# Weighing the low-rank product of a language-model tower: one VectorE product against a ScalarE copy and a GpSimd product, with GpSimd's normalising behind VectorE's gate

## The chip, the core and the metric

The kernel runs on one core of a Trainium2 chip. The time is the device time of one execution in microseconds (us), taken as the median of several runs. The engines are called by their names or by the profile's short ones: PE is TensorE (matmuls; PEld its weight loads), DVE is VectorE, ACT is ScalarE, POOL is GpSimd, and SP is SyncE, which here only issues DMAs.

## What is computed

32 sequences of 512 tokens, width 128, everything in float32. The embedding of the tokens gives h; then h = h + attention(layernorm(h)) with 8 heads of width 16, and h = h + experts(layernorm(h)). The change sits in the experts. Cut to what matters, with xf the normalised input (`softmax` over the 4 experts e):

```python
gate_logits = softmax(xf @ gate_w.T)
adapted = gate_logits - sigmoid(xf @ thr_w.T) / e
weights = adapted * (adapted >= 0)
weights = weights / sum(weights)                  # 1 where the sum is 0
hidden = relu(einsum('ni,ehi->neh', xf, fc1_w))
lo = einsum('neh,ehr->ner', hidden, lora_A)       # rank 16 for each expert
lo = einsum('ner,ero->neo', lo, lora_B)
out = einsum('ne,ned->nd', weights, einsum('neo,edo->ned', lo, fc2_w))
```

## The kernel before

`tower` keeps one pipeline going over the 32 sequences. Each engine has its own program, and all of them walk through the same steps t = -5 to 34. In step t the attention scores of sequence t are made, while other sequences are in other stages: the work that belongs to sequence t+k is listed with its offset k. So (-3) is the end of the experts of sequence t-3, (-2) the gate and the first expert product of t-2, (-1) the last part of the attention of t-1, (+3) the queries and keys of t+3.

A step has 16 slots c. PE does in each slot two score tiles for the softmax (`scores_T`, L724, into a ring `sc` of 3 PSUM banks), two score tiles whose row maxima are wanted ahead of time (`scores`, L750, into `mix`, 4 PSUM banks), one product from the table `PRODUCTS`, and in every fourth slot 16 matmuls with the values (`values`, L737). Its order is fixed by `PE_ORDER`. The low-rank product `low` (L809) is that of slot 3, the turning `xn2T` (L762) that of slot 5, and the experts' output `out` (L825) that of slot 6. A bank of `mix` is written again four uses later, and PE waits there for whoever reads it last (`mix_user`, `mix_free`). A bank of the ring is written three tiles later, when ACT's exponential of the tile before has been done (`ring_free`).

The other engines follow tables that say after which tile of the step each piece of work stands, and each engine executes in that order:

- ACT (`ACT_WORK`): 32 exponentials (`exp`, L592) a step. Ahead of the one of slot 4 stand the bias and the bfloat16 cast of the queries and of the keys of t+3 (`copy_qk`, L596 and L600, four instructions) and the copy of the second half of the attention's result of t-1 (`copy_ctx`, L616).
- DVE (`DVE_WORK`): 32 row maxima (`row_max`, L1025) a step. In slot 3 stand the embedding's add, half of its statistics and `weigh` (L1099), which reads the low-rank product from PSUM, multiplies it by the gate weights `wrow` and writes `low`. In slot 7 stand `finish` (L1104), the last add of sequence t-3, and `invert_den` (L1044), the reciprocal of the softmax's denominators of t-1. In slots 9 and 10 stands the gate of t-2: some ten small instructions between SBUF tiles, of which `gsm` (L1071), `gad` (L1074), `gsel` (L1080), `wsafe` (L1087) and the last, `wts` (L1092), are named below.
- POOL (`POOL_WORK`): among others `norm2` (L491, L495), then five products that cut the queries and keys into three bfloat16 pieces (`second`, L485, comes first), then `normalise` (L528 twice, L532), which multiplies the attention's result by the reciprocals.
- SP (`SP_WORK`) issues the DMAs in one queue. Those of interest go ahead of each other in this order: two pieces of 128 KB (L339), the denominators out to DRAM (`den_out`, L369), a third piece, the denominators back in (`den_in`, L385), ..., the reciprocals out and in again (`rden_out`, `rden_in`, L392 and L400), ..., and at the end of the step `stack`, the six loads of queries and keys of t+3 from DRAM (L356, L363), some 1.5 MB.

The chain of the denominators therefore is, within one step: `values` of slot 3, `copy_ctx` on ACT, `den_out`, `den_in`, `invert_den` on DVE, `rden_out`, `rden_in`, `normalise` on POOL, and in the next step's slot 0 the product `project` (L787) on PE.

A wait is written `upto(engine, semaphore, b, n)`: until n signals have come for every sequence up to b.

## Time and profile before

| | |
|---|---|
| median of 3 runs | 1127.43 us (1126.55 to 1129.59) |
| the profiled execution's own time | 1126.86 us |
| its span, first to last instruction | 1125.1 us |
| PE busy | 1040.1 us, 92% |
| DVE busy | 948.8 us, 84% |
| ACT busy | 807.0 us, 72% |
| POOL busy | 682.1 us, 61% |
| mean granted PE clock | 0.962 of full speed |

The profile is that of one execution. Starts are counted from the start of the span. A row of the timeline may join several like instructions (x4); what stands in brackets behind it is the time in which the engine was idle before it, and what ended that wait.

### The profile page before, as it was taken

Reading aid. Unit: us, or ns where it says so; the run is one execution under the profiler, and the core shown is the slowest. Engines: PE = TensorE matmul, PEld = TensorE weight load, DVE = VectorE, ACT = ScalarE, POOL = GpSimd, SP = SyncE. Lnnn points to the kernel's source line nnn. Section 1 sums busy time; section 2 is a strip of 40 time slices with the busy share of each in tenths; the row PEclk is TensorE's granted clock in tenths of the full one; section 3 lists DMA queues with packets and bytes.
Section 4 is the critical chain, followed back from the end, with each engine's and each line's share of the span. In section 5 each row is a group of like instructions: output and inputs, shape, how many; then the busy total and the mean of one; then the engine's idle time right before and its main releaser. Section 6 shows DMA issues by size and latency. Waiting matters only on the chain.

```text
span 1125.1 us, 20263 instructions
## 1 busy us (share of the span) xinstructions
PE 1040.1 (92%) x6158; PEld 407.9 (36%) x6158; DVE 948.8 (84%) x2442; ACT 807.0 (72%) x1578; POOL 682.1 (61%) x684
## 2 busy tenths in 40 slices
PE   4368999999999999999999999999999999989865
PEld 2112233333434434343433443434343343333322
DVE  7498899999989989899999999999999998887312
ACT  2217787777877788787877778778787777856731
POOL 1855676677666666677666666667766666621231
PEclk9558999999999999999999999999999999999997
DMA  2553645555554445555555545565555554541111
GB/s 74 148 135 89 137 106 135 129 137 127 137 130 124 126 121 130 142 127 134 126 137 126 126 121 132 130 143 126 137 125 137 128 126 113 121 96 36 55 50 32
DMA packets 93530, 132.43 MB, mean 118 GB/s; under 512 B 18205, under 2 KB 69918, under 8 KB 87398
## 3 DMA queue, kind: packets, MB, share of 16 engines
q1 hardware_dynamic: 91872, 129.54, 47.9%
q10 hardware_dynamic: 1550, 1.59, 0.6%
q8 instruction: 50, 0.82, 0.3%
q14 instruction: 58, 0.48, 0.1%
HBM read 89.20 MB, written 35.01 MB: 110 GB/s over the span
## 4 chain that ended last, share of the span: by engine, by line
PE 64%; DVE 16%; DMA 6%; ACT 5%; issue 2%; POOL 1%; SPq 1%; POOLq 0%; ACTq 0%; DVEq 0%
PE pv L737 17%; PE mix L750 15%; PE sc L724 13%; DVE negmax L1025 9%; PE mix L804 7%; DMA den_dram<-ctx_sb 4%; PE mix L787 3%; DVE bn L1015 2%; ACT probs L592 2%; PE mix L809 2%; DVE h L1050 2%; PE mix L825 2%; DMA den<-den_dram 2%; ACT qk L596 1%; PE mix L769 1%
## 5 line engine op out<-in xcount | busy, mean ns | idle before, releaser
L1025 DVE TENSOR_REDUCE negmax<-mix 128x1 f32<-128x512 f32 x1024 | 649.0, 679 | 56.8 <-PE mix L750 56.2
L592 ACT ACTIVATE probs<-sc 128x512 f32<-128x512 f32 x1024 | 556.3, 600 | 118.2 <-PE sc L724 112.0
L724 PE MATMUL sc<-qstk,kstk 120*128 120x512 bf16 x1024 | 364.2, 382 | 5.6 <-ACT probs L592 4.9
L750 PE MATMUL mix<-kstk,qstk 96*128 96x512 bf16 x1024 | 331.7, 395 | 24.6 <-DMA kstk<-stack_dram 7.3
L737 PE MATMUL pv<-probs,vals 128*32 128x512 f32 x2048 | 244.8, 595 | 0.0
L528 POOL TENSOR_TENSOR ctxh<-ctx_sb,rdenb 128x512 f32<-128x512 f32 x64 | 81.0, 1268 | 245.3 <-DMA rdenb<-rden_dram 244.5
L750 PEld LDWEIGHTS mix<-kstk,qstk 96*128 96x128 bf16 x1024 | 89.4, 98 | 266.5 <-DVE negmax L1025 76.1
L724 PEld LDWEIGHTS sc<-qstk,kstk 120*128 120x128 bf16 x1024 | 100.1, 98 | 107.5 <-ACT probs L592 33.4
L804 PE MATMUL mix<-xn2T,fc1T_sb 128*128 128x512 f32 x256 | 138.2, 622 | 0.7 <-ACT hid L646 0.7
L508 POOL TENSOR_TENSOR qk<-qk,rstdb 128x512 f32<-128x512 f32 x64 | 81.1, 1269 | 57.9 <-DMA rstdb<-rstd_dram 53.4
L737 PEld LDWEIGHTS pv<-probs,vals 128*32 128x32 f32 x2048 | 59.1, 109 | 117.4 <-issue 100.1
L646 ACT ACTIVATE hid<-mix 128x512 f32<-128x512 f32 x128 | 76.5, 598 | 31.2 <-PE mix L804 28.7
L502 POOL TENSOR_TENSOR pieces<-qkr,pieces 128x512 bf16<-128x512 f32 x64 | 74.0, 1156 | 8.5
L485 POOL TENSOR_TENSOR pieces<-qk,pieces 128x512 bf16<-128x512 f32 x64 | 74.0, 1156 | 6.6 <-ACT pieces L600 6.6
L479 POOL TENSOR_TENSOR qkr<-qk,pieces 128x512 f32<-128x512 f32 x64 | 74.1, 1159 | 0.0
L460 POOL TENSOR_TENSOR rstd<-ve,minus_half 128x4 f32<-128x4 f32 x64 | 64.9, 1013 | 5.0
L458 POOL TENSOR_TENSOR ve<-mv,eps_sb 128x4 f32<-128x4 f32 x64 | 12.9, 201 | 73.8 <-DVE mv L1021 71.1
L804 PEld LDWEIGHTS mix<-xn2T,fc1T_sb 128*128 128x128 f32 x256 | 43.9, 191 | 36.7 <-DVE negmax L1025 24.7
L605 ACT COPY v<-mix 128x512 f32<-128x512 f32 x32 | 18.8, 586 | 46.8 <-POOL vals L520 39.1
L474 POOL TENSOR_TENSOR hb_sb<-h_sb,obias 128x512 f32<-128x512 f32 x32 | 40.5, 1265 | 15.0 <-DVE h L1050 14.8
L1010 DVE TENSOR_TENSOR qk<-mix,posQK 128x512 f32<-128x512 f32 x64 | 43.4, 679 | 7.1 <-POOL qkr L479 6.6
L1050 DVE TENSOR_TENSOR h<-mix,hb_sb 128x512 f32<-128x512 f32 x32 | 22.1, 692 | 28.6 <-PE mix L787 27.5
(141 smaller groups left out, 1088.5 us busy)
## 6 DMA issues: line engine op xcount, KB each, us to landing
stack_dram<-pieces SPq DMA_DIRECT2D x192, 128.0 KB
rdenb<-rden_dram SPq DMA_DIRECT2D x64, 256.0 KB
qstk<-stack_dram SPq DMA_DIRECT2D x31, 384.0 KB, 6.6
kstk<-stack_dram SPq DMA_DIRECT2D x31, 384.0 KB, 8.8
rstdb<-rstd_dram SPq DMA_DIRECT2D x32, 256.0 KB, 3.4
wrow<-w_dram SPq DMA_DIRECT2D x32, 256.0 KB
out<-out_sb SPq DMA_DIRECT2D x32, 256.0 KB, 2.6
qstk<-stack_dram SPq DMA_DIRECT2D x31, 256.0 KB, 7.0
```

The source lines that it names most:

```text
L479: pool.tensor_tensor(qkr[:, side, :], qk32[:, side, :], pieces[:, side, 0, :], ALU.subtract).then_inc(s_res0, 1)
L485: pool.tensor_tensor(pieces[:, side, 1, :], qk32[:, side, :], pieces[:, side, 0, :], ALU.subtract).then_inc(s_pc1, 1)
L502: pool.tensor_tensor(pieces[:, side, 2, :], qkr[:, side, :], pieces[:, side, 1, :], ALU.subtract).then_inc(s_pc2, 1)
L508: pool.tensor_tensor(qk32[:, side, :], qk32[:, side, :], rstdb[:], ALU.mult).then_inc(s_scaled, 1)
L528: pool.tensor_tensor(ctxh[:, g, :], ctx_sb[:, u % 2, g, :], rdenb[:, g, :], ALU.mult).then_inc(s_ctxh, 1)
L592: act.activation(probs[:, c % 8, i % 2], sc[:, i % RING], ACT.Exp).then_inc(s_exp, 1)
L646: act.activation(hid[:, e, :], aux(f"fc1_{e}", 1), ACT.Relu).then_inc(s_hid, 1)
L724: pe.matmul(sc[:, i % RING, :], kstk[0:KROWS, u, h, j * P:(j + 1) * P], qstk[0:KROWS, u, h, :], start=True, stop=True).then_inc(s_score, 1)
L737: mm = pe.matmul(pv[Q * i:Q * i + Q, :], vals[:, u, 2 * half + jj, 4 * g + i, :], probs[:, 4 * (r % 2) + i, jj, :], start=(half == 0 and j ...
L750: pe.matmul(max_bank(m), qstk[0:STK, u, h, j * P:(j + 1) * P], kstk[0:STK, u, h, :], start=True, stop=True).then_inc(s_mxmm, 1)
L804: pe.matmul(aux(f"fc1_{e}", 1), fc1T_sb[:, e, :], xn2T[:], start=True, stop=True).then_inc(s_fc1mm, 1)
L1025: dve.tensor_reduce(negmax[:, m // NT, m % NT:m % NT + 1], max_bank(m), AX.X, ALU.max, negate=True).then_inc(s_max, 1)
```

## The change

VectorE's `weigh` goes. ScalarE gets `copy_low` ahead of the queries' bias in slot 4: it copies the low-rank product from PSUM to `low`. GpSimd gets `weigh` behind `norm2`: it multiplies `low` in place by `wrow`. The new semaphore `s_lowcp` stands between the two, and PE's wait for the bank of `mix` that held the product is now on it. Apart from that, `normalise` of sequence b on GpSimd now first waits until the gate of b-1 is complete on VectorE (13 signals), except for the last sequence. The rest of the arithmetic and all DMAs are the same.

```diff
--- before.py
+++ after.py
@@ -61,7 +61,7 @@
 BEFORE, BEHIND = (3, 7), (11,)
 
 ACT_WORK = [
-    (1, 1, "relu", -3, 3), (4, 0, "qk", 3, 0), (4, 0, "qk", 3, 1), (4, 0, "ctx", -1, 1), (6, 0, "xn2T", -2, 0),
+    (1, 1, "relu", -3, 3), (4, 0, "low", -3, 0), (4, 0, "qk", 3, 0), (4, 0, "qk", 3, 1), (4, 0, "ctx", -1, 1), (6, 0, "xn2T", -2, 0),
     (8, 0, "gates", -2, 0), (9, 1, "gate_exp", -2, 0), (9, 1, "relu", -2, 0), (10, 1, "relu", -2, 1),
     (12, 0, "rT", 4, 0), (12, 0, "wT", -2, 0), (12, 0, "mT", 1, 0), (12, 1, "ctx", 0, 0), (13, 1, "relu", -2, 2),
     (15, 2, "v", 4, 0),
@@ -69,14 +69,14 @@
 
 DVE_WORK = [
     (0, 1, "add_attention", -2, 0), (1, 0, "stats2", -2, 0), (1, 1, "stats2", -2, 1), (2, 0, "moments2", -2, 0),
-    (3, 1, "add_pos", 4, 0), (3, 1, "stats1", 4, 0), (3, 1, "weigh", -3, 0), (6, 0, "stats1", 4, 1),
+    (3, 1, "add_pos", 4, 0), (3, 1, "stats1", 4, 0), (6, 0, "stats1", 4, 1),
     (6, 1, "moments1", 4, 0), (7, 1, "finish", -3, 0), (7, 1, "invert_den", -1, 0),
     (9, 0, "gate", -2, 0), (10, 1, "gate", -2, 1), (10, 1, "gate", -2, 2), (10, 1, "gate", -2, 3),
     (13, 0, "add_qk", 4, 0), (15, 1, "add_qk", 4, 1), (15, 1, "hot", 5, 0),
 ]
 
 POOL_WORK = [
-    ("scale", 3, 0), ("add_bias", 3, 0), ("scale", 3, 1), ("rstd2", -2, 0), ("norm2", -2, 0),
+    ("scale", 3, 0), ("add_bias", 3, 0), ("scale", 3, 1), ("rstd2", -2, 0), ("norm2", -2, 0), ("weigh", -3, 0),
     ("second", 3, 0), ("residual", 3, 0), ("third", 3, 0), ("second", 3, 1), ("rstd1", 4, 0),
     ("residual", 3, 1), ("third", 3, 1), ("normalise", -1, 0), ("v", 3, 0),
 ]
@@ -287,6 +287,7 @@
         s_wTmm, s_wT, s_wout, s_win = sem("s_wTmm"), sem("s_wT"), sem("s_wout"), sem("s_win")
         s_fc1mm, s_hid = sem("s_fc1mm"), sem("s_hid")
         s_lomm, s_low = sem("s_lomm"), sem("s_low")
+        s_lowcp = sem("s_lowcp")
         s_outmm, s_out, s_store = sem("s_outmm"), sem("s_out"), sem("s_store")
 
         def upto(eng, s, b, per=1, k=None):
@@ -523,6 +524,8 @@
 
             def normalise(b, u):
 
+                if b < NSEQ - 1:
+                    upto(pool, s_gate, b - 1, 13)
                 for g in range(2):
                     upto(pool, s_rdin[g], b, 16)
                     pool.tensor_tensor(ctxh[:, g, :], ctx_sb[:, u % 2, g, :], rdenb[:, g, :],
@@ -531,6 +534,11 @@
                 upto(pool, s_projmm, b - 1)
                 pool.tensor_tensor(ctxn[:], ctxh[:, 0, :], ctxh[:, 1, :], ALU.add).then_inc(s_ctxn, 1)
 
+            def weigh(b):
+                upto(pool, s_lowcp, b)
+                upto(pool, s_win, b, 16)
+                pool.tensor_tensor(low[:], low[:], wrow[:], ALU.mult).then_inc(s_low, 1)
+
             pool.wait_ge(s_setcp, 4)
             pool.wait_ge(s_const, 3)
 
@@ -539,6 +547,7 @@
                 "rstd2": lambda b, u, _: rstd_second(b),
                 "scale": lambda b, u, side: scale(b, side),
                 "v": lambda b, u, _: value(b, u),
+                "weigh": lambda b, u, _: weigh(b),
                 "residual": lambda b, u, side: residual(b, side),
                 "second": lambda b, u, side: second(b, side),
                 "third": lambda b, u, side: third(b, side),
@@ -635,6 +644,11 @@
                 upto(act, s_wout, b - 1, 16 * WREP)
                 act.copy(wT, aux("mT", 1)[Q:Q + NT * NE, 0:P]).then_inc(s_wT, 1)
 
+            def copy_low(b):
+                upto(act, s_lomm, b)
+                upto(act, s_outmm, b - 1)
+                act.copy(low[:], aux("low", 1)).then_inc(s_lowcp, 1)
+
             def copy_rT(b):
                 upto(act, s_rTmm, b)
                 upto(act, s_rstdout, b - 1, 16)
@@ -651,6 +665,7 @@
                 "xn2T": lambda b, u, _: copy_xn2T(b),
                 "relu": lambda b, u, e: relu(b, e),
                 "wT": lambda b, u, _: copy_wT(b),
+                "low": lambda b, u, _: copy_low(b),
                 "rT": lambda b, u, _: copy_rT(b),
                 "mT": lambda b, u, _: copy_mT(b),
                 "ctx": lambda b, u, g: copy_ctx(b, g, u),
@@ -837,7 +852,7 @@
                 "fc1_2": (lambda b: fc1(b, 2), (s_hid, NE, 3)),
                 "fc1_3": (lambda b: fc1(b, 3), (s_hid, NE, 4)),
                 "embed": (embed, (s_h, 1, 1)),
-                "low": (low_rank, (s_low, 1, 1)),
+                "low": (low_rank, (s_lowcp, 1, 1)),
                 "mT": (turn_max, (s_mT, 1, 1)),
                 "project": (project, (s_h2, 1, 1)),
                 "out": (experts_out, (s_out, 1, 1)),
@@ -1092,12 +1107,6 @@
                 dve.tensor_tensor(wts[:, 0:NT], gsel[:], wrec[:].unsqueeze(2).broadcast_to([P, NT, NE]),
                                   ALU.mult).then_inc(s_gate, 1)
 
-            def weigh(b):
-                upto(dve, s_lomm, b)
-                upto(dve, s_win, b, 16)
-                upto(dve, s_outmm, b - 1)
-                dve.tensor_tensor(low[:], aux("low", 1), wrow[:], ALU.mult).then_inc(s_low, 1)
-
             def finish(b, u):
                 upto(dve, s_outmm, b)
                 upto(dve, s_store, b - 1, 16)
@@ -1119,7 +1128,6 @@
                 "stats2": lambda b, u, half: stats(b, h2[:, b % H2], bn2, s_h2, s_bn2, half),
                 "moments2": lambda b, u, _: moments(b, bn2, mv2, s_bn2, s_mv2),
                 "gate": lambda b, u, part: (gate_first, gate_second, gate_third, gate_fourth)[part](b),
-                "weigh": lambda b, u, _: weigh(b),
                 "finish": lambda b, u, _: finish(b, u),
             }
```

ACT, in a step of the steady part, from the end of slot 3 to slot 4 (L592 and L601 are the exponentials, L596/L605 and L600/L609 the queries' and keys' bias and cast, L616/L625 `copy_ctx`). Before:

```order
L592 ACTIVATE probs<-sc 128x512 x5
L596 ACTIVATE qk<-qk,qb_sb 128x512
L600 CAST pieces<-qk 128x512
L596 ACTIVATE qk<-qk,qkb_sb 128x512
L600 CAST pieces<-qk 128x512
L616 COPY ctx_sb<-pv 128x512
L592 ACTIVATE probs<-sc 128x512 x4
L621 COPY xn2T<-mix 128x512
```

And with the change:

```order
L601 ACTIVATE probs<-sc 128x512 x5
L650 COPY low<-mix 128x512
L605 ACTIVATE qk<-qk,qb_sb 128x512
L609 CAST pieces<-qk 128x512
L605 ACTIVATE qk<-qk,qkb_sb 128x512
L609 CAST pieces<-qk 128x512
L625 COPY ctx_sb<-pv 128x512
L601 ACTIVATE probs<-sc 128x512 x4
L630 COPY xn2T<-mix 128x512
```

The new copy stands ahead of four instructions for the queries and keys, of `copy_ctx` and of the exponentials of slot 4 and later.

POOL, the middle of a step (L495/L496 is the end of `norm2`, L528/L531 and L532/L535 are `normalise`). Before:

```order
L491 TENSOR_TENSOR xn<-h,mv 128x512
L495 TENSOR_TENSOR xn<-xn,rstd 128x512
L485 TENSOR_TENSOR pieces<-qk,pieces 128x512
L479 TENSOR_TENSOR qkr<-qk,pieces 128x512
L502 TENSOR_TENSOR pieces<-qkr,pieces 128x512
L485 TENSOR_TENSOR pieces<-qk,pieces 128x512
L458 TENSOR_TENSOR ve<-mv,eps_sb 128x4
L460 TENSOR_TENSOR rstd<-ve,minus_half 128x4
L479 TENSOR_TENSOR qkr<-qk,pieces 128x512
L502 TENSOR_TENSOR pieces<-qkr,pieces 128x512
L528 TENSOR_TENSOR ctxh<-ctx_sb,rdenb 128x512 x2
```

And with the change:

```order
L492 TENSOR_TENSOR xn<-h,mv 128x512
L496 TENSOR_TENSOR xn<-xn,rstd 128x512
L540 TENSOR_TENSOR low<-low,wrow 128x512
L486 TENSOR_TENSOR pieces<-qk,pieces 128x512
L480 TENSOR_TENSOR qkr<-qk,pieces 128x512
L503 TENSOR_TENSOR pieces<-qkr,pieces 128x512
L486 TENSOR_TENSOR pieces<-qk,pieces 128x512
L459 TENSOR_TENSOR ve<-mv,eps_sb 128x4
L461 TENSOR_TENSOR rstd<-ve,minus_half 128x4
L480 TENSOR_TENSOR qkr<-qk,pieces 128x512
L503 TENSOR_TENSOR pieces<-qkr,pieces 128x512
L531 TENSOR_TENSOR ctxh<-ctx_sb,rdenb 128x512 x2
```

Eight instructions, and with them the pieces' stores on SP, come after the new product.

## Rows read from the trace of the kernel before

**Rows 1.** The page: busy time of each engine (us, share, instructions)
```profile
PE 1040.1 (92%) x6158; PEld 407.9 (36%) x6158; DVE 948.8 (84%) x2442; ACT 807.0 (72%) x1578; POOL 682.1 (61%) x684
```
**Rows 2.** Timeline of PE, `low` in six steps: start, us, what [idle before]
```profile
176.16 1.06 PE L809 MATMUL mix<-hid,loA_sb 128*32 128x512 f32 x8
...
490.18 1.06 PE L809 MATMUL mix<-hid,loA_sb 128*32 128x512 f32 x8
...
521.35 1.06 PE L809 MATMUL mix<-hid,loA_sb 128*32 128x512 f32 x8
...
553.02 1.06 PE L809 MATMUL mix<-hid,loA_sb 128*32 128x512 f32 x8
...
991.24 1.07 PE L809 MATMUL mix<-hid,loA_sb 128*32 128x512 f32 x8
...
1026.03 1.06 PE L809 MATMUL mix<-hid,loA_sb 128*32 128x512 f32 x8
```
**Rows 3.** Timeline of DVE, the reciprocal in two of those steps
```profile
500.23 0.35 DVE L1044 RECIPROCAL rden<-den 128x32 f32<-128x32 f32 x1 [0.70 <-DMA den<-den_dram]
...
532.07 0.35 DVE L1044 RECIPROCAL rden<-den 128x32 f32<-128x32 f32 x1 [1.35 <-DMA den<-den_dram]
```
**Rows 4.** Timeline of all engines, slots 3 and 4 of one step
```profile
615.69 1.07 PE L809 MATMUL mix<-hid,loA_sb 128*32 128x512 f32 x8
...
616.43 0.72 ACT L596 ACTIVATE qk<-qk,qb_sb 128x512 f32<-128x512 f32 x1
...
617.66 1.04 POOL L495 TENSOR_TENSOR xn<-xn,rstd 128x512 f32<-128x512 f32 x1
...
617.87 0.67 DVE L1099 TENSOR_TENSOR low<-mix,wrow 128x512 f32<-128x512 f32 x1
...
618.83 3.16 DVE L1025 TENSOR_REDUCE negmax<-mix 128x1 f32<-128x512 f32 x5 [0.29 <-PE mix L750]
...
618.99 0.58 ACT L616 COPY ctx_sb<-pv 128x512 f32<-128x512 f32 x1
...
619.47 2.21 ACT L592 ACTIVATE probs<-sc 128x512 f32<-128x512 f32 x4
...
619.84 0.52 SPq L369 DMA_DIRECT2D den_dram<-ctx_sb  x1
...
620.67 0.38 PE L724 MATMUL sc<-qstk,kstk 120*128 120x512 bf16 x1
...
621.54 1.05 PE L825 MATMUL mix<-exp_w,low 128*128 128x128 f32 x8
```
**Rows 5.** The page's groups: `normalise`'s two products, busy and mean ns | idle before
```profile
L528 POOL TENSOR_TENSOR ctxh<-ctx_sb,rdenb 128x512 f32<-128x512 f32 x64 | 81.0, 1268 | 245.3 <-DMA rdenb<-rden_dram 244.5
```
**Rows 6.** Timeline of SP, `stack`'s last loads and the denominators in two steps
```profile
611.44 1.58 SPq L363 DMA_DIRECT2D kstk<-stack_dram  x3
...
624.46 0.34 SPq L385 DMA_DIRECT2D den<-den_dram  x1
...
994.70 0.56 SPq L369 DMA_DIRECT2D den_dram<-ctx_sb  x1
998.75 0.34 SPq L385 DMA_DIRECT2D den<-den_dram  x1
```
**Rows 7.** The chain that ended last, the denominators' store in step 32
```profile
1082.72 1.69 DMA den_dram<-ctx_sb
```
**Rows 8.** Timeline, gate against `normalise` in step 29 (and the last row in step 30)
```profile
1007.20 2.58 POOL L528 TENSOR_TENSOR ctxh<-ctx_sb,rdenb 128x512 f32<-128x512 f32 x2 [12.94 <-DMA rdenb<-rden_dram]
1007.23 1.27 DVE L1071 TENSOR_TENSOR gsm<-lexp,grec 128x16 f32<-128x16 f32 x1
...
1011.63 0.41 PE L814 MATMUL mix<-id,wts 128*32 128x128 f32 x2 [2.62 <-DVE wts L1092]
...
1043.99 0.41 PE L814 MATMUL mix<-id,wts 128*32 128x128 f32 x2 [0.85 <-DVE wts L1092]
```
**Rows 9.** Timeline of DVE, `weigh` in the last step
```profile
1118.73 0.69 DVE L1099 TENSOR_TENSOR low<-mix,wrow 128x512 f32<-128x512 f32 x1 [7.41 <-DMA wrow<-w_dram]
```

## The prediction

> **What bounds the kernel now.** I read the busy shares first. PE is at 92% and DVE at 84%, ACT and POOL far below [rows 1], so PE sets the pace and the question is what still makes it wait. A 26-step stretch of the pipeline runs from `low` of step 3 to `low` of step 29: 991.24 - 176.16 = 815.1 us, or 31.35 us a step [rows 2].
>
> Then I compared steps. `low` to `low` is 31.17 in one step and 31.67 in the next [rows 2]. Eight of the 26 steps lie within 0.01 of 31.18, and none is shorter: a floor. The reciprocal of the denominators begins 500.23 - 490.18 = 10.05 after `low` in the step at the floor, and 532.07 - 521.35 = 10.72 in the long one [rows 2, 3]. DVE idles for the denominators in both, 0.70 and 1.35 [rows 3]. So a step lasts 31.18, and longer by what the reciprocal comes later than about 10.72 - 0.50 = 10.22. Two things can therefore lengthen a step: PE's own stream, and the chain of the denominators. Spare time elsewhere buys nothing.
>
> **DVE loses `weigh`: worth nothing.** 32 x 0.67 us = 21.5 us of DVE work go [rows 4]. But behind it DVE idles 0.29 us until PE delivers the next score tile [rows 4], and before the reciprocal it idles again [rows 3]. Without `weigh` the first of these gaps grows to about 0.96, and the row maxima start at the same moment. The bank of `mix` comes free earlier (about 617.4 against 618.54), but PE wants it only for the second row-max tile of slot 4, after 619. I cost the removal at zero. If that cover were gone, it would be worth up to 26 x 0.17 = 4.4 us, the excess over the floor.
>
> The Trainium skill says otherwise, in "Perfetto Trace Analysis", section "Optimizing Scalar/DVE Operations": where DVE is saturated, moving work to Scalar or even GPSIMD may pay. It would make this edit a gain, and is the third rival below. The 0.29 us of idle time behind `weigh` speak against DVE being saturated here.
>
> **ACT gains a copy, at a bad place.** `low` ends at 616.76 on PE; DVE's response to PE is some hundredths, so the copy starts at about 616.82, where the queries' bias started at 616.43 [rows 4]. A copy of this shape holds ACT for 619.47 - 618.99 = 0.48 before the next instruction starts [rows 4]. Everything behind it then starts at 617.30, later by 0.86. Two customers are behind it.
>
> First, PE's ring. The exponential of slot 4 would start at 620.33 and, with some 0.60 for one of them, end at 620.93; PE needs that for the score tile that it now starts at 620.67 [rows 4]. That tile comes at about 620.99: 0.32 later, less than the 0.86 because the ring had slack. The next tiles need later exponentials and fit behind the shifted stream. PE's stream from here to the reciprocal shows no wait in which 0.32 could vanish, so I let the floor rise to 31.50. Over 26 steps that is at least 26 x (0.32 - 0.17) = 3.9 us, more in the five steps that already lie above 31.50 (the denominators set their length, so they gain nothing and lose nothing; by their excess over 31.50, 0.7 in all): **+4.6 us**. Bounds: 0 if PE absorbs it, 26 x 0.32 = 8.3 if the two delays add.
>
> Second, `copy_ctx` and with it `den_out`, which would be issued at 620.70 instead of 619.84. Here I had to choose. `den_in` follows it after 624.46 - 619.84 = 4.62 us [rows 4, 6]. In step 32, without other traffic, the same store takes 1.69 [rows 7]. So some 2.9 us of the 4.62 are waiting in the DMA queues, behind the six big loads issued until 613.0 [rows 6] and two pieces. Step 29 separates the causes: no pieces are stored there, `den_out` goes out at 3.46 after `low` instead of 4.15, and still `den_in` comes only at 998.75 - 991.24 = 7.51 instead of 8.77 [rows 2, 4, 6]. Its latency, 4.05, is still far above 1.69, so the backlog of the loads sets the landing, not the issue. With the later issue the store would still be queued before that backlog is gone (620.70 + 1.69 = 622.4, against 624.46). I take a shift of **0** for the landing; the other end is the full 0.86, which the rivals price.
>
> The Trainium skill's "DMA: Bandwidth & Descriptors", section "Anatomy of one DMA", speaks against this choice: a fixed cost of about 2 us, most of it the write receipt from the target, plus bytes over bandwidth. By that a store of 8 KB lands a constant time after its issue, so 0.86 later, and the sum would be that of the first rival. The unloaded 1.69 agrees with the page, the 4.62 and 4.05 do not.
>
> **POOL gains a product, in idle time.** It costs 1.27 us like the two-input product of `normalise` [rows 5]. `norm2` ends at 618.70, so it runs until about 619.97, and its input, the copy, is there by 617.4. `out` on PE starts at 621.54 [rows 4]: 1.5 us to spare. The cutting of the pieces moves 1.27 later, and the first of the POOL pieces goes to SP behind `den_out`, ahead of `den_in`: it would be ready at about 621.2 and issued before 622, still before 624.46. POOL then waits for the reciprocals, 244.5 us in all over 32 sequences, 7.6 a step [rows 5]; the 1.27 come out of that. If the cover were gone, it would be 26 x 1.27 = 33 us. I cost it at zero.
>
> **POOL's `normalise` waits for the gate.** In the steady steps the reciprocals arrive after the gate is done, so the wait costs nothing, or a few tenths that `project` does not feel. In steps 29 and 30 it is the other way round. No pieces delay the denominators there, `normalise` starts in the middle of the gate, and the gate's `gsm` takes 1.27 us, exactly the time of POOL's product beside it [rows 8]. PE then waits 2.62 for the gate's result, and 0.85 in step 30 [rows 8]. Step 29 lasts 1026.03 - 991.24 = 34.79, 3.61 above the floor [rows 2], although it lacks the products `q`, `k`, `v` and `embed`. Behind the wait those two steps should be clean. I take -4.0 for step 29 (between 2.6, PE's wait alone, and some 4.5, the excess plus the missing products) and -0.85 for step 30: **-4.9 us**. `normalise` itself moves by 1.5 us there, and `project` follows only in the next step.
>
> **The drain.** In the last step `weigh` starts when its weights land [rows 9] and PE waits for it: 1.27 - 0.69 = +0.6. In the two steps before, `weigh` on POOL stands behind `norm2`, and `out` on PE stands between the turning and the gate's matmuls; it comes between 0 and 0.7 later, since only the turning's matmuls are beside the product. I take 0.35 twice. **+1.3 us**. In steps 29 to 31 ACT has no queries and keys to cast and waits for PE there, so the copy is covered.
>
> **Sum:** 4.6 - 4.9 + 1.3 = +1.0 us. The profiled execution took 1126.86 us (span 1125.1 and 1.8 around it), which gives 1127.9. That execution lies 0.57 below the median of the three runs, so for a median I say 1128.4.
>
> **Rivals.**
>
> 1. The denominators land 0.86 later. The queue is not what holds the small store, or the later pieces push into a gap in front of it. Then DVE's reciprocal moves from a mean of about 10.3 to 11.1 after `low`, and a step lasts 31.18 + 0.9 = 32.1 instead of 31.35: 26 x 0.73 = +19, in all 19.0 - 4.9 + 1.3 = +15.4, or 1143. It decides from a shift of the landing of some 0.1 us on. For it: in both rows the landing is later in the step where the store is issued later. Against it: the backlog above.
> 2. The gate's wait gives nothing, because the collision moves instead of going, or the tail is short of something else. Then +4.9 comes back: 1133. Against it: the overlap is exactly what the wait forbids.
> 3. The relief counts and ACT's copy is absorbed. The ring's stall does not appear: 0 - 4.9 + 1.3 = -3.6, or 1124. If the missing `weigh` also lets DVE run ahead and takes the 4.4 us of excess with it, 1119.5. For it: DVE is busy 84% [rows 1]. Against it: the 0.29, and that the reciprocal waits for a DMA.
> 4. The change does less than it says: the queries' bias starts hardly later (ACT overlaps the copy with it), and the collisions in the tail had their cause in the load of that one execution, not in the order. Then nothing is left but the drain, +1.3: 1129.
>
> **Chances.** My forecast with cases around it 0.50 (its own range 1124 to 1133); rival 1 0.15; rival 2 0.08; rival 3 0.22; rival 4 0.05. A measurement of this kernel can tell about 0.3%, 3.4 us, from no change: 1124.0 to 1130.8 is the same. Of the forecast 0.34 lies inside, 0.05 below and 0.11 above; of rival 3 0.17 below and 0.05 inside; rival 4 inside; rivals 1 and 2 above. That gives faster 0.22, same 0.44, slower 0.34. The range leaves out no more than 2 in 10: it runs from 1120, which drops the lower form of rival 3, to 1140, which drops most of rival 1's full form.
>
> **What would show it.** The floor of `low` to `low` at about 31.5 instead of 31.18, with PE's score tile of slot 5 at 5.3 after `low` instead of 4.98. `den_out` near 5.0 after `low`, but `den_in` still at 8.4 to 8.8. DVE idle for about 0.95 us before the row maxima of slot 3. POOL's product ending near 4.3, with `out` unmoved apart from the 0.3. No gate instruction longer than some 0.2 us, and step 29 at about 31. A `den_in` near 9.5 would prove rival 1, an unchanged floor rival 3.

## The result and the profile after

The changed kernel takes 1133.31 us (median of 6 runs, 1131.26 to 1134.42), the kernel before beside it 1127.38 (1125.41 to 1129.59): a ratio of 1.0051, 95% interval [1.0037, 1.0065]. It is slower by half a per cent. That lies in the range (1120 to 1140), 4.9 us above the forecast and just outside what I had called the same.

The page's line on the engines shows the change as planned: DVE lost 24.5 us of work, POOL gained 37.6 and ACT 11.6 (against [rows 1]).

```profile
PE 1046.3 (92%) x6158; PEld 406.3 (36%) x6158; DVE 924.3 (82%) x2410; ACT 818.6 (72%) x1610; POOL 719.7 (64%) x716
```

The timeline of PE, `low` in six steps (start, us, what), answers to [rows 2]:

```profile
176.24 1.07 PE L824 MATMUL mix<-hid,loA_sb 128*32 128x512 f32 x8
...
460.82 1.06 PE L824 MATMUL mix<-hid,loA_sb 128*32 128x512 f32 x8
...
493.31 1.06 PE L824 MATMUL mix<-hid,loA_sb 128*32 128x512 f32 x8
...
524.82 1.07 PE L824 MATMUL mix<-hid,loA_sb 128*32 128x512 f32 x8
...
1001.12 1.07 PE L824 MATMUL mix<-hid,loA_sb 128*32 128x512 f32 x8
...
1031.89 1.07 PE L824 MATMUL mix<-hid,loA_sb 128*32 128x512 f32 x8
```

The 26 steps take 1001.12 - 176.24 = 824.9 us where they took 815.1. A step at the floor lasts 524.82 - 493.31 = 31.51, and the long one ahead of it 493.31 - 460.82 = 32.49. Step 29 is down from 34.79 to 30.77. Of every trace I took this sum, the same way:

| profiled execution | 26 steps | of it 26 floors | above the floor | step 29 | step 30 | from `low` of step 31 on | span |
|---|---|---|---|---|---|---|---|
| before | 815.1 | 810.7 | 4.4 | 34.79 | 29.42 | 69.6 | 1125.1 |
| after | 824.9 | 819.3 | 5.6 | 30.77 | 28.33 | 72.4 | 1132.6 |
| difference | +9.8 | +8.6 | +1.2 | -4.0 | -1.1 | +2.8 | +7.5 |

(The start up to the first `low` is 0.1 later. The profiled execution of after, 1134.42 by its own time, is 1.1 above its median.)

The timeline of all engines over slots 3 and 4 of the step whose `low` starts at 620.40, against [rows 4]:

```profile
620.40 1.07 PE L824 MATMUL mix<-hid,loA_sb 128*32 128x512 f32 x8
...
621.53 0.59 ACT L650 COPY low<-mix 128x512 f32<-128x512 f32 x1 [0.28 <-PE mix L824]
...
622.02 0.72 ACT L605 ACTIVATE qk<-qk,qb_sb 128x512 f32<-128x512 f32 x1
...
622.37 1.04 POOL L496 TENSOR_TENSOR xn<-xn,rstd 128x512 f32<-128x512 f32 x1
...
623.37 1.27 POOL L540 TENSOR_TENSOR low<-low,wrow 128x512 f32<-128x512 f32 x1
...
623.54 2.48 DVE L1040 TENSOR_REDUCE negmax<-mix 128x1 f32<-128x512 f32 x4 [0.89 <-PE mix L765]
...
624.57 0.58 ACT L625 COPY ctx_sb<-pv 128x512 f32<-128x512 f32 x1
...
625.42 0.52 SPq L370 DMA_DIRECT2D den_dram<-ctx_sb  x1
...
625.71 0.39 PE L739 MATMUL sc<-qstk,kstk 120*128 120x512 bf16 x1 [0.17 <-ACT probs L601]
...
626.59 1.05 PE L840 MATMUL mix<-exp_w,low 128*128 128x128 f32 x8
...
628.35 0.34 SPq L386 DMA_DIRECT2D den<-den_dram  x1
```

Relative to `low`: the queries' bias starts at 1.62 (before 0.74), `copy_ctx` at 4.17 (3.30), `den_out` at 5.02 (4.15), PE's score tile at 5.31 (4.98) and `out` at 6.19 (5.85). Ahead of that tile PE now waits for an exponential; the view gives 0.17 of idle time for it, the tile itself starts 0.33 later. `den_in` goes out at 7.95 here, at 8.37 in the mean of the 26 steps (before 8.48). DVE idles 0.89 ahead of the row maxima (before 0.29).

Two steps differ in the reciprocal, in DVE's timeline:

```profile
472.35 0.35 DVE L1059 RECIPROCAL rden<-den 128x32 f32<-128x32 f32 x1 [1.83 <-DMA den<-den_dram]
...
503.18 0.35 DVE L1059 RECIPROCAL rden<-den 128x32 f32<-128x32 f32 x1 [0.17 <-DMA den<-den_dram]
```

The first comes 11.53 after its `low`, the second 9.87. The DMA view of 469.5 to 472.4, in the long step (queue, kind: packets, MB, share; then an issue with KB and us to landing), shows what differs:

```profile
q8 instruction: 1, 0.02, 2.3%
...
den<-den_dram SPq DMA_DIRECT2D x1, 16.0 KB, 2.8
```

And of 501.4 to 503.2, in the step at the floor; it has no line for q8:

```profile
den<-den_dram SPq DMA_DIRECT2D x1, 16.0 KB, 1.7
```

The same read of the denominators takes 2.8 us to land in the one and 1.7 in the other. The one has beside its read a packet of queue 8, 16 KB of instructions, that starts at 470.09; the other has none. The page counts 50 of these packets in 1132.6 us. A narrower DMA view, 470.05 to 470.25, holds this packet and nothing else, with this share of 16 engines' 0.2 us, which is 1.05 us on one of them:

```profile
q8 instruction: 1, 0.02, 32.7%
```

The 50 packets of this trace take 0.88 to 2.06 us, 1.14 in the mean.

The read gives 16 landing signals, one for each part of it. In the long step 15 of them have come by 1.60 us after the issue, and the last comes at 2.82. It is so in all eight steps of the 26 that have such a packet beside the read: 14 of the 16 are there by 1.65, and the last comes at 2.00 to 3.39. In the other 18 steps the last comes at 1.54 to 1.81. What is late is one part of the read, in one step two, and not the whole.

The gate in step 29, against [rows 8], in the timeline: `normalise` starts when `wts` is done, the gate's `gsm` takes 0.18 instead of 1.27, and PE's turning stands there without a wait.

```profile
1017.11 0.18 DVE L1086 TENSOR_TENSOR gsm<-lexp,grec 128x16 f32<-128x16 f32 x1
...
1018.59 0.30 PE L829 MATMUL mix<-id,wts 128*32 128x128 f32 x1
1018.61 2.49 POOL L531 TENSOR_TENSOR ctxh<-ctx_sb,rdenb 128x512 f32<-128x512 f32 x2 [13.25 <-DVE wts L1107]
```

The last step, against [rows 9]: the weights land, POOL's product takes 1.26 instead of 0.69, and PE waits 4.10 instead of 3.0.

```profile
1125.72 1.26 POOL L540 TENSOR_TENSOR low<-low,wrow 128x512 f32<-128x512 f32 x1 [14.89 <-DMA wrow<-w_dram]
1127.13 2.04 PE L840 MATMUL mix<-exp_w,low 128*128 128x128 f32 x8 [4.10 <-POOL low L540]
```

### The profile page after: what moved, and what is told of

Read it like the earlier page. It is cut to its first block, busy times and chain, and to the rows that moved or that the text cites. A ratio compares the mean times of both kernels' runs of the same rounds, so it can differ in the third digit from the quotient of the medians.

```text
span 1132.6 us, 20356 instructions
## 1 busy us (share of the span) xinstructions
PE 1046.3 (92%) x6158; PEld 406.3 (36%) x6158; DVE 924.3 (82%) x2410; ACT 818.6 (72%) x1610; POOL 719.7 (64%) x716
## 4 chain that ended last, share of the span: by engine, by line
PE 59%; DVE 15%; ACT 8%; DMA 5%; issue 5%; POOL 2%; SPq 1%; POOLq 0%; ACTq 0%
PE pv L752 14%; PE mix L765 13%; PE sc L739 12%; DVE negmax L1040 9%; PE mix L819 8%; ACT qk L605 4%; PE mix L824 3%; PE mix L802 3%; DMA den_dram<-ctx_sb 2%; ACT probs L601 2%; DVE bn L1030 2%; PE mix L840 2%; DMA den<-den_dram 2%; DVE h L1065 2%; PE mix L784 1%
## 5 line engine op out<-in xcount | busy, mean ns | idle before, releaser
L601 ACT ACTIVATE probs<-sc 128x512 f32<-128x512 f32 x1024 | 550.3, 603 | 124.2 <-PE sc L739 121.5
L765 PE MATMUL mix<-kstk,qstk 96*128 96x512 bf16 x1024 | 330.3, 394 | 26.9 <-DVE negmax L1040 7.8
L531 POOL TENSOR_TENSOR ctxh<-ctx_sb,rdenb 128x512 f32<-128x512 f32 x64 | 80.4, 1266 | 212.5 <-DMA rdenb<-rden_dram 144.5
L765 PEld LDWEIGHTS mix<-kstk,qstk 96*128 96x128 bf16 x1024 | 88.4, 98 | 268.4 <-DVE negmax L1040 78.2
L540 POOL TENSOR_TENSOR low<-low,wrow 128x512 f32<-128x512 f32 x32 | 40.7, 1271 | 14.9 <-DMA wrow<-w_dram 14.9
L1113 DVE TENSOR_TENSOR out_sb<-mix,h 128x512 f32<-128x512 f32 x32 | 21.8, 682 | 32.3 <-PE mix L840 32.3
```

Source lines behind the costliest of these rows:

```text
L531: pool.tensor_tensor(ctxh[:, g, :], ctx_sb[:, u % 2, g, :], rdenb[:, g, :], ALU.mult).then_inc(s_ctxh, 1)
L601: act.activation(probs[:, c % 8, i % 2], sc[:, i % RING], ACT.Exp).then_inc(s_exp, 1)
L765: pe.matmul(max_bank(m), qstk[0:STK, u, h, j * P:(j + 1) * P], kstk[0:STK, u, h, :], start=True, stop=True).then_inc(s_mxmm, 1)
```

## The experiments

My theory after the result: the ScalarE copy costs all of it, by the floor and by late reads of the denominators; the gate's wait is a gain; GpSimd's product costs only in the drain; VectorE's relief is worth nothing. The rivals: the delay is one of the denominators' landing; the relief counts; the product has a part in the steady steps. The first four runs split the change, the next four cross its parts and test the late reads, and the last two test the relief. In the cuts of code, `...` stands for what is left out. Ratios are to the kernel before on the same chip (its median was 1127.16 for the first four, 1128.62 for the next, 1127.87 for the last two).

**The wait alone (`gate_only`).**

```diff
             def normalise(b, u):
 
+                if b < NSEQ - 1:
+                    upto(pool, s_gate, b - 1, 13)
                 for g in range(2):
```

> The kernel before, with only the normalising's wait for the gate. Theory (the collision in steps 29 and 30 is what the wait removes): step 29 falls from 34.79 to about 30.8 us, step 30 from 29.42 to about 28.3, all steps before stay at their floor of 31.18, so the time is 4 to 5 us shorter, some 1122.5. Rival (the tail was short of something else): no change, 1127.4.

Measured: 1120.98, ratio 0.9938 [0.9919, 0.9957]. 6 to 7 us faster than before, so this part alone beats both kernels. Its floor is 31.18, the 26 steps take 813.2, step 29 30.75. Step 30 took 29.97, not 28.33. The same kernel, measured again below, gave 0.9950 and 28.34.

**The copy alone (`act_copy`).** ScalarE copies in slot 4, VectorE's `weigh` multiplies the copy.

```diff
-    (1, 1, "relu", -3, 3), (4, 0, "qk", 3, 0), ...
+    (1, 1, "relu", -3, 3), (4, 0, "low", -3, 0), (4, 0, "qk", 3, 0), ...
...
+            def copy_low(b):
+                upto(act, s_lomm, b)
+                upto(act, s_outmm, b - 1)
+                act.copy(low[:], aux("low", 1)).then_inc(s_lowcp, 1)
...
             def weigh(b):
-                upto(dve, s_lomm, b)
+                upto(dve, s_lowcp, b)
```

> The kernel before, with only ScalarE's copy of the product at the place where the change has it; VectorE's weigh stays and overwrites the copy, no GpSimd product, no wait for the gate. Theory A (the copy's place lengthens the floor through the ring of score banks): floor 31.52 instead of 31.18, score tile of slot 5 at 5.30 after low. If the late reads of the denominators, seen in 7 steps of the changed kernel, also come from ScalarE's delay of the pieces: about 9 us slower, 1136 to 1137. If they come from GpSimd's product ahead of the third piece: only 4 to 5 us slower, 1132.

Measured: 1141.16, ratio 1.0121 [1.0095, 1.0147]. Slower than either value that I had named. The floor is 31.51, as in the changed kernel, so the copy alone raises it. The late reads are there too (11 of the 26 steps have a fetch of instructions beside the read). But four steps last 32.8 to 33.6, which the changed kernel doesn't have. There I had overlooked something; the crossing below shows what.

**The copy on VectorE (`dve_copy`).** The changed kernel, with its copy not on ScalarE but on VectorE, at `weigh`'s old place.

```diff
-    ... (4, 0, "low", -3, 0), (4, 0, "qk", 3, 0), ...
+    ... (4, 0, "qk", 3, 0), ...
...
-    (3, 1, "add_pos", 4, 0), (3, 1, "stats1", 4, 0), (6, 0, "stats1", 4, 1),
+    (3, 1, "add_pos", 4, 0), (3, 1, "stats1", 4, 0), (3, 1, "low", -3, 0), (6, 0, "stats1", 4, 1),
...
-                act.copy(low[:], aux("low", 1)).then_inc(s_lowcp, 1)
...
+                dve.tensor_copy(low[:], aux("low", 1)).then_inc(s_lowcp, 1)
```

> The changed kernel with the copy made by VectorE in the old place of weigh instead of by ScalarE; GpSimd's product and the wait for the gate stay. Theory A: floor back at 31.18, score tile of slot 5 at 4.98, tail still 5 us better, drain still some 2.5 us worse: 1124 to 1125 if the late reads of the denominators come from ScalarE, up to 1130 if they come from GpSimd's product.

Measured: 1123.99, ratio 0.9971 [0.9956, 0.9986]. The floor is back at 31.17 and the score tile at 4.98, with GpSimd's product still there; the 26 steps take 815.1. From `low` of step 31 on it takes 72.9, as long as in the changed kernel (72.4).

**The copy later (`late_copy`).** The changed kernel with the copy behind `copy_ctx`, and POOL's `weigh` behind its first piece.

```diff
-    ... (4, 0, "low", -3, 0), (4, 0, "qk", 3, 0), (4, 0, "qk", 3, 1), (4, 0, "ctx", -1, 1), ...
+    ... (4, 0, "qk", 3, 0), (4, 0, "qk", 3, 1), (4, 0, "ctx", -1, 1), (4, 0, "low", -3, 0), ...
...
-    ... ("norm2", -2, 0), ("weigh", -3, 0),
-    ("second", 3, 0), ...
+    ... ("norm2", -2, 0),
+    ("second", 3, 0), ("weigh", -3, 0), ...
```

> The changed kernel with ScalarE's copy moved behind the queries, the keys and the attention copy, and GpSimd's product behind the first of the pieces' products. Theory A: exponential of slot 4 only 0.48 later, which the ring's slack of about 0.6 covers: floor 31.18, den_out back at 4.15 after low; with the tail's gain and the drain's loss about 1124 to 1125. Rival (any instruction more on ScalarE costs its length): 26 x 0.48 = 12 us more than that, 1137.

Measured: 1135.08, ratio 1.0061 [1.0044, 1.0078]. A miss: `den_out` is back at 4.15, but the floor rose to 31.72. The timeline of this kernel, in the step whose `low` starts at 620.02, shows the wait that took its place:

```profile
623.31 0.58 ACT L625 COPY ctx_sb<-pv 128x512 f32<-128x512 f32 x1
623.79 0.59 ACT L650 COPY low<-mix 128x512 f32<-128x512 f32 x1
...
624.43 0.60 PE L765 MATMUL mix<-kstk,qstk 96*128 96x512 bf16 x2 [0.66 <-ACT low L650]
```

PE wants the bank of `mix` that holds the product for a row-max tile, and waits 0.66 for the copy, 17.8 us in all 28 such steps by the page's group of L765. So neither of the two places tried in slot 4 of ScalarE is free: in front the copy delays the exponential, behind `copy_ctx` it delays PE's bank. A place after some of the slot's exponentials wasn't tried.

**The parts crossed (`act_gate`, `no_gate`).** The first is the copy alone plus the wait; that is the change without GpSimd's product. The second is the changed kernel without the wait:

```diff
             def normalise(b, u):
 
-                if b < NSEQ - 1:
-                    upto(pool, s_gate, b - 1, 13)
                 for g in range(2):
```

> The kernel before with ScalarE's copy and with the wait of `normalise`, but with VectorE's `weigh` in its place (it multiplies the copy): the change without GpSimd's product. Theory (the product itself costs nothing in the steady steps, and the long steps of the run with the copy alone came from `normalise` beside a late gate): floor 31.52, no step above 32.6, late reciprocals as in the changed kernel, and a drain without GpSimd's 1.3 to 2.7: 1130.5 to 1132.5. Rival (GpSimd's product takes the place of VectorE's for a gain, or the row maxima behind `weigh` are late): above 1135, as with the copy alone.

Measured: 1132.60, ratio 1.0027 [1.0013, 1.0040].

> The changed kernel without the wait of `normalise`: ScalarE's copy and GpSimd's product alone. If the wait is worth only what it saves in the steps 29 and 30, 5.1: 1138.4. If it also holds `normalise` off the gate in the steady steps, as the long steps of the run with the copy alone suggest (four steps above 32.6 there): 1140 to 1142. If nothing collides since VectorE is ahead without `weigh`: 1133, as with the wait.

Measured: 1145.22, ratio 1.0148 [1.0125, 1.0172], more than any of the values named. All parts together, the wait alone with both of its measurements (`gate_only`, `gate_only2`):

| wait | copy | product | ratio | 26 steps | step 29 | step 30 | from step 31 on |
|---|---|---|---|---|---|---|---|
| | | | 1 | 815.1 | 34.79 | 29.42 | 69.6 |
| x | | | 0.9938 | 813.2 | 30.75 | 29.97 | 69.9 |
| x | | | 0.9950 | 814.7 | 30.77 | 28.34 | 69.9 |
| | x | | 1.0121 | 828.8 | 33.71 | 30.84 | 69.9 |
| x | x | | 1.0027 | 825.6 | 30.78 | 28.33 | 69.8 |
| | x | x | 1.0148 | 834.7 | 33.53 | 30.19 | 71.5 |
| x | x | x | 1.0051 | 824.9 | 30.77 | 28.33 | 72.4 |

The intervals of the ratios are 0.0013 to 0.0026 to either side, so a difference of two of them is known to some 2 to 4 us.

- GpSimd's product: 0.0024 to 0.0027 of 1127, some 3 us, which is hardly more than that uncertainty. The traces tell more. With the wait, the 26 steps are as long with the product as without it (824.9, 825.6), and from step 31 on all six kernels with it take 71.5 to 72.9 and the five executions with VectorE's product instead 69.6 to 69.9.
- ScalarE's copy: with the wait 1.0027 - 0.9938 = 0.0089 or 1.0027 - 0.9950 = 0.0077, so 9 to 10 us.
- The wait: 0.0050 to 0.0062, or 6 to 7 us, without the copy, and 0.0094 to 0.0097, or 11 us, with it.

Rows of `no_gate` in step 11, in the middle of the steady part, show why the wait is worth more with the copy:

```profile
450.09 1.26 POOL L529 TENSOR_TENSOR ctxh<-ctx_sb,rdenb 128x512 f32<-128x512 f32 x1 [4.99 <-DMA rdenb<-rden_dram]
450.12 1.26 DVE L1105 TENSOR_TENSOR wts<-gsel,wrec 128x16 f32<-128x16 f32 x1
451.43 0.11 PEld L827 LDWEIGHTS mix<-id,wts 128*32 128x32 f32 x1 [0.97 <-DVE wts L1105]
451.43 0.30 PE L827 MATMUL mix<-id,wts 128*32 128x128 f32 x1 [0.79 <-DVE wts L1105]
```

The reciprocals land while the gate's last product is due. POOL starts 0.03 us earlier, `wts` lasts 1.26 instead of 0.17, PE waits 0.79, and the step lasts 32.62. The last gate instruction starts 17.56 after `low` in the changed kernel's steps at the floor, 17.23 in the kernel before, while `normalise` can start at 17.30 (its earliest in `no_gate`) or 17.52 (in the kernel before). The margin of 0.1 is gone with the copy. And where the reciprocal is late, the gate, behind it on DVE, is late with it: the steps of 33.2 to 34.0 in `no_gate` all have a reciprocal at 11.4 or later. The groups of `no_gate` (busy us, mean ns | idle before):

```profile
L1105 DVE TENSOR_TENSOR wts<-gsel,wrec 128x16 f32<-128x16 f32 x32 | 14.1, 441 | 1.1
L1100 DVE SCALAR_TENSOR_TENSOR wsafe<-wsum 128x4 f32<-128x4 f32 x32 | 7.9, 248 | 1.1
...
L827 PE MATMUL mix<-id,wts 128*32 128x128 f32 x64 | 12.9, 283 | 11.1 <-DVE wts L1105 11.1
```

And those of the changed kernel:

```profile
L1107 DVE TENSOR_TENSOR wts<-gsel,wrec 128x16 f32<-128x16 f32 x32 | 5.6, 174 | 1.1
L1102 DVE SCALAR_TENSOR_TENSOR wsafe<-wsum 128x4 f32<-128x4 f32 x32 | 5.2, 162 | 1.1
...
L829 PE MATMUL mix<-id,wts 128*32 128x128 f32 x64 | 13.0, 284 | 1.0 <-DVE wts L1107 1.0
```

With the wait of `normalise`, PE's waiting for `wts` is 11.1 - 1.0 = 10.1 us shorter. Of the 11.1 us, 4.1 lie in the steps 29 and 30, where the kernel before waits too (3.5), and 4.8 in six of the 26 steps, where the kernel before never waits. How much the collision lengthens those six can be told from the steps beside them: where nothing collides, a late reciprocal sets the length (at 11.43 after `low` 32.39, at 11.59 32.56, so 20.96 more than its start). By that the six steps are 6.2 us too long. So the collision explains 6.2 of the 9.8 us by which the 26 steps are longer than in the changed kernel (834.7, 824.9). The rest is that more reciprocals are late: `no_gate` has 11 steps with a fetch packet beside the read, the changed kernel 8. Whether the missing wait has a part in that wasn't tested.

The Trainium skill, "SBUF — State Buffer", section "Who interferes with whom", says that a VectorE instruction with two inputs in SBUF and a GpSimd one that reads SBUF exclude each other for the whole of the one that started first. The rows agree: `wts`, which starts 0.03 behind POOL's product, ends 0.03 behind it.

**Padding (`after_pad20`, `after_pad37`).** To move the fetches of instructions, PE got 20 or 37 more waits ahead of its first matmul:

```diff
             pe.wait_ge(s_emb_w, 16 * 5)
+            nc.disable_value_cache = True
+            for _ in range(20):
+                pe.wait_ge(s_emb_w, 16 * 5)
+            nc.disable_value_cache = False
```

> The changed kernel with 20 more PE instructions ahead of the loop (waits that are already met), so that every later fetch of PE's instructions (a packet of 16 KB on queue 8, about 256 instructions) comes 20 instructions, some 1.7 us, earlier against the pipeline. Theory (the late reciprocals come from a fetch packet between 8.8 and 9.7 after `low`, in the way of the read of the denominators): those packets now fall near 7.1 to 8.0, the steps longer than 31.6 go from seven to at most two, and the time falls by 3 to 5 us, to about 1128 to 1130. Rival (the fetches only coincide with late reads, and the later ScalarE stream itself makes the reads late): seven long steps stay and the time is 1133.

> The same with 37 more instructions. The fetches recur every 256 PE instructions and a step has some 365, so seven steps are nearly ten fetches and the phases of the fetches lie some 37 instructions apart: a shift by 37 gives each phase to another step and leaves the set of phases as it was. Theory: about as many steps longer than 31.6 as in the changed kernel (five to eight), in other steps, and 1132 to 1134. Rival (added waits help by something else, such as the start): the time falls as with 20.

Measured: 1135.20, ratio 1.0044 [1.0030, 1.0058], and 1137.24, ratio 1.0063 [1.0044, 1.0082]. With 20 waits nothing is gained. In the compiled program two such waits make one instruction, so the shift was 19 instead of 37 (and about 10 instead of 20); and the fetches stayed where they were in the step: in groups at about 4, 9, 14, 20.5 and 25.5 after `low`, one of them between 8.7 and 9.5 in 11 and 10 of 27 steps. (A step has 401 PE instructions in the trace, not 365; seven steps are then nearly eleven fetches, and the phases still lie some 37 apart.) When a fetch lands isn't set by PE's place in its program alone; what does set it stays open. So the cause isn't tested by this pair.

What the pair and the other traces give is a count. Over all twelve traces (with those of the last two runs, below) the reciprocal starts 1.6 to 2.2 us after `den_in` where no fetch packet starts near the read, and 1.9 to 3.6 after it where one does (from 0.3 ahead of `den_in` to 1.6 behind), and there, in all but two cases, 2.0 to 2.7 after the packet's start:

| traces | fetch packets beside the read, of 26 steps | their mean start after `low` | mean start of the reciprocal there |
|---|---|---|---|
| no copy on ScalarE in slot 4 (5 traces) | 5 to 7 | 8.4 to 8.5 | 10.5 to 10.7 |
| copy ahead of the queries (6 traces) | 8 to 11 | 9.0 to 9.1 | 11.0 to 11.3 |
| copy behind `copy_ctx` (`late_copy`) | 5 | 9.1 | 11.0 |

In the other steps the reciprocal starts at 9.9 to 10.2 in the mean of each trace, with or without the copy. The time above the floor follows this: in the changed kernel the 8 steps with a packet hold 5.3 us of the 5.6, in the kernel before 5 steps hold 1.9 of the 4.4. And in all twelve traces 14 of the read's 16 landing signals come by 1.8 us, with a packet beside it or without. That a later ScalarE stream alone makes the read late does not fit: the steps without a packet read as fast with the copy as without it. Whether the packet holds up the late part, or something else holds up both, stays open.

**No weighing (`no_weigh`).** `gate_only` without the product on any engine; the experts' output isn't computed.

```diff
-    (3, 1, "add_pos", 4, 0), (3, 1, "stats1", 4, 0), (3, 1, "weigh", -3, 0), (6, 0, "stats1", 4, 1),
+    (3, 1, "add_pos", 4, 0), (3, 1, "stats1", 4, 0), (6, 0, "stats1", 4, 1),
...
-                upto(sp, s_low, b - 1)
+                upto(sp, s_win, b - 1, 16)
...
-                upto(pe, s_low, b)
+                pe.wait_ge(s_low, 1)
...
-                "low": (low_rank, (s_low, 1, 1)),
+                "low": (low_rank, (s_lomm, 1, 1)),
...
+            dve.memset(low[:], 0.0).then_inc(s_low, 1)
```

> The kernel before with the wait of `normalise` alone, once more, on the chip of the next kernel, for the comparison with it and because it is the fastest so far: 1120 to 1122 where the kernel before has 1127, a ratio of 0.992 to 0.996.

Measured: 1122.76, ratio 0.9950 [0.9933, 0.9967]. 26 steps 814.7, step 30 28.34.

> The same without any weighing: VectorE's product is left out and nobody does it, `low` holds zeros that are written once, so the experts' output is not computed. VectorE has 32 x 0.67 us less to do, ScalarE and GpSimd nothing more: the relief of the change alone. Theory (relief is worth nothing in the steady steps): the floor stays at 31.18 and the 26 steps take 812 to 816 us, as with the product (813.2); only the last step, in which PE waited for the weights and the product, is up to 4 us shorter: 1117 to 1121. Rival (VectorE runs ahead and the time above the floor goes, or the floor falls): below 810 for the 26 steps, and below 1116 in all.

Measured: 1119.57, ratio 0.9924 [0.9904, 0.9945]. 26 steps 815.8, floor 31.19. The relief of 21.5 us is worth nothing in the steady part. The two medians lie 3.2 us apart, and the last step is 3.9 shorter: from its `low` to the end 5.6 us instead of 9.5. PE doesn't wait 2.93 for the weights and the product, and the eight matmuls of `out` take 0.9 less. The timelines of that `out`, of `gate_only2` first:

```profile
1114.56 0.69 DVE L1101 TENSOR_TENSOR low<-mix,wrow 128x512 f32<-128x512 f32 x1 [7.33 <-DMA wrow<-w_dram]
...
1115.40 2.05 PE L827 MATMUL mix<-exp_w,low 128*128 128x128 f32 x8 [2.93 <-DVE low L1101]
```

And of `no_weigh`:

```profile
1112.97 1.16 PE L828 MATMUL mix<-exp_w,low 128*128 128x128 f32 x8
```

## Why the prediction was right, and where not

The range held, and so did most of the structure. Of the six terms the three zeros held, as far as the traces can tell (two executions of one kernel, `gate_only`, differ by 1.5 us in the 26 steps), the gate's wait came out within 0.3 us, and the other two were too small. The range was 20 us wide; the case that I held likeliest ended at 1133, and the measured median lies just above that.

- **DVE's relief, 0.** Right, and shown by `no_weigh`. DVE's idle time ahead of the row maxima grew to 0.89 (said: about 0.96), and without any weighing the floor stays at 31.19. This answers rival 3, as does the raised floor.
- **The floor, 31.50.** Measured 31.51, with the score tile at 5.31 (said: 5.3). `act_copy` and `dve_copy` show that ScalarE's copy in this place costs this, and not the product: with VectorE's copy the floor is 31.17.
- **The price of the floor, +4.6.** This is the term that was mis-sized: it measured +9.8. The step that failed is that steps already longer than 31.50 "gain nothing and lose nothing", since the denominators set their length, so that 26 x 0.17 of the rise would vanish in the old excess. The floor alone gave 26 x 0.33 = 8.6, already more than my upper bound of 8.3, and the excess went from 4.4 to 5.6 instead of falling to 0.7. (The rise alone says little, since the two executions of `gate_only` have 2.6 and 3.6; but it didn't fall.) The excess is of two kinds. In the steps without a fetch packet beside the read it fell from 2.5 to 0.4, as the argument wants. In those with one it rose from 1.9 (5 steps) to 5.3 (8 steps): the packets start some 0.6 later after `low` with the copy, more of them fall beside the read, and the reciprocal moves along with them. I had taken all of it for one tail of the landings, fixed in time. That the lateness goes with the packets is shown; that they cause it is not.
- **The landing of the denominators, shift 0.** Right: with the store issued 0.87 later, `den_in` goes out at 8.37 instead of 8.48 in the mean. Rival 1 needed 9.5. The Trainium skill ("DMA: Bandwidth & Descriptors", section "Anatomy of one DMA — SWDGE (gpsimd) path") gives its nearly constant cost for DMAs that GpSimd issues. This store is issued by SP, which the prediction didn't say, and a constant doesn't describe it: from `den_out` to `den_in` it was 4.3 in the mean before and 3.3 now. What came late is the read behind it, by one of its 16 parts.
- **POOL's product in idle time, 0.** Right in the steady steps (`act_gate`; in `dve_copy`, with the product, they take 815.1, as before); it came out of the wait for the reciprocals, as said.
- **The gate's wait, -4.9.** In the steps 29 and 30 it measured -4.0 and -1.1. But "in the steady steps the wait costs nothing" left out that it might give something there. It does, since the copy closes the margin between the gate and `normalise`: without the wait the 26 steps are 9.8 longer, some 6.2 of it by the collision. Against the kernel before, which had the margin, that is no gain, so the sum is untouched; but taken alone I would have priced the wait's absence at 5 and it was 11. Rival 2 had it the wrong way round.
- **The drain, +1.3.** It measured +2.8. I had counted the longer product, 0.6 in the last step. There it was 1.1 (10.66 from `low` to the end instead of 9.57), since the weights also land later, 3.76 after `low` instead of 3.24; why they do stays open. The other 1.7 lie in the two steps before, where I had counted 0.7. In one of them PE also works slower. From 1108 to 1122 the windows view gives PE a granted clock of 0.64 and 10.51 us of busy time for 39 matmuls, where the kernel before has 0.87 and 9.07 for 39 in the like stretch. Of after, then of before (window, length, busy us of PE, PEld, DVE, ACT, POOL, granted clock, DMA share, GB/s):

```profile
1108.00:1122.00 14.00, 10.51 (x39) 4.81 (x37) 2.73 (x14) 4.30 (x9) 2.69 (x3) 0.64 0.07 20
```

```profile
1101.00:1115.00 14.00, 9.07 (x39) 4.45 (x39) 3.42 (x15) 3.41 (x9) 3.17 (x4) 0.87 0.07 20
```

Four matmuls of `fc1` take 3.64 us in that stretch, at the lower level of 1.2 GHz, and 1.94 before, at 2.4. But the lower clock is neither peculiar to the change nor most of its loss in the drain. From `low` of step 33 to that of step 34, `gate_only` has 0.73 without the product, and its drain takes 69.9; `no_gate` has 0.89 with the product, and its drain takes 71.5:

```profile
1094.63:1109.10 14.47, 10.18 (x40) 4.71 (x41) 3.42 (x15) 3.72 (x8) 3.07 (x3) 0.73 0.07 20
```

```profile
1120.76:1135.60 14.84, 9.07 (x40) 3.95 (x40) 2.74 (x14) 4.30 (x9) 4.51 (x5) 0.89 0.07 19
```

The sum by the traces: 9.8 - 5.1 + 2.8 = +7.5 in the profiled executions, +5.9 in the medians; predicted +1.0. The likeliest case, "same", had 0.44, and slower 0.34. What happened is nearest to the forecast's own upper bound, where the delays add, and a little above it.

## What to carry to other kernels

Split a change with several parts before judging it: here a wait worth 6 to 7 us was wrapped in a copy that cost 9 to 10, and the wait alone gives 0.994 to 0.995 of the time before. When a pipeline's steps have a floor and an excess, don't let a rise of the floor eat the excess unless you know what causes the excess; look which of its steps move with the pipeline. And an in-order engine that looks idle by its share (ACT at 72%) can still have no free place ahead of the instruction that the bound engine waits for.

## What the runs showed of the hardware

- A fetch of PE's instructions is a DMA packet of 16 KB (50 in the changed kernel, 0.88 to 2.06 us each, 1.14 in the mean). A small read that is due at the same time lands up to 1.9 us late: the reciprocal behind it starts 1.6 to 2.2 us after its issue where no packet starts near it, and 1.9 to 3.6 where one does. Only one or two of its 16 parts are late. It was seen in all twelve traces; it hasn't been shown by moving the packets, which the padding failed to do.
- Those packets gather at the same places of each step and hardly move with the number of instructions ahead (some 10 and 19 more).
- The last `out`, eight matmuls, took 2.05 us behind a wait of PE of 2.93 (`gate_only2`; granted clock from that step's `low` to the end 0.62) and 1.16 where PE didn't wait (`no_weigh`; 1.00).
- With the same code one profiled execution (`gate_only`) had step 30 at 29.97 and another (`gate_only2`) at 28.34, so a difference of 1.6 us in one such step need not come from a change.
